# A two-layer megakernel on 2048 tokens: the last chunk of 512 split into two of 256

## What is computed

```
x = ln(x + mamba(x))                    # recurrence of 256 channels x 16 states along each sequence
x = ln(x + fp8_linear(x))
x = ln(x + ssm(x))                      # recurrence of 16 states, one delta per token
x = ln(x + moe(x))                      # 8 experts, top 2, capacity 512 per expert, plus a side net

def mamba(x):
    xi, res = split(x @ in_proj.T)
    xi = silu(causal_conv4(xi))
    dt, B, C = split(xi @ x_proj.T)
    delta = softplus(dt @ dt_proj.T + b)
    h[t] = exp(delta[t] * A) * h[t-1] + delta[t] * B[t] * xi[t]      # per channel and state
    y = sum over states of h[t] * C[t] + xi * D
    return (y * silu(res)) @ out_proj.T

def moe(x):                             # every expert is applied to every token here,
    h = rms(x)                          # and weighted with its routing weight, mostly zero
    out_e = (gelu(h @ Wg[e]) * (h @ Wu[e])) @ Wd[e]
```

## Time and profile before

| | us |
|---|---|
| median of 3 runs | 455.78 |
| lowest and highest run | 454.69, 455.82 |
| the profiled execution, its own time | 457.87 |
| its span, first to last instruction | 456.1 |
| mean granted TensorE clock | 0.945 of full speed |
| busy: TensorE, VectorE | 406.6 (89%), 380.9 (84%) |
| busy: ScalarE, GpSimd | 316.4 (69%), 257.7 (57%) |
| table loads of ScalarE | 66, 84.7 in all |

### The profile page before, as it was taken

The page is one execution under the profiler, slowest core; times in us unless marked ns, Lnnn a source line. Parts: engine busy times, 40 slices in busy tenths (PEclk is TensorE's granted clock), DMA queues, the critical chain, the costliest instruction groups (busy, mean ns, idle before and its releaser), DMA issues.

```text
span 456.1 us, 6082 instructions
## 1 busy us (share of the span) xinstructions
PE 406.6 (89%) x1700; PEld 245.5 (54%) x1700; DVE 380.9 (84%) x849; ACT 316.4 (69%) x524; POOL 257.7 (57%) x230
## 2 busy tenths in 40 slices
PE   9969977688676999999999899999978998999993
PEld 5323422243223568866354477675434865868872
DVE  3599998999998999999999899999897566657654
ACT  2787637267954768887889999899672779566331
POOL 0348899999899744766865199978592000000000
PEclk9988989799789799999999899999988999999997
DMA  8397597786773925655652852757440000000000
GB/s 264 144 384 264 213 324 308 278 290 220 239 251 124 283 91 181 198 171 185 216 176 92 266 207 90 276 185 227 166 138 0 2 1 0 1 2 23 1 0 23
DMA packets 22208, 74.18 MB, mean 163 GB/s; under 512 B 2336, under 2 KB 4512, under 8 KB 21792
## 3 DMA queue, kind: packets, MB, share of 16 engines
q1 hardware_dynamic: 22176, 73.82, 47.8%
HBM read 72.50 MB, written 1.31 MB: 162 GB/s over the span
## 4 chain that ended last, share of the span: by engine, by line
PE 61%; DVE 15%; ACT 14%; issue 9%; POOL 1%; DVEq 0%; ACTq 0%; POOLq 0%
PE ps_y L659 14%; PE ps_net L753 14%; PE ps_acc L799 9%; DVE ps_state L1263 4%; DVE product L1280 3%; PE ps_net L619 3%; ACT ps_state L945 3%; PE ps_state L753 3%; ACT L817 2%; PE ps_y L799 2%; PE ps_net L624 1%; PE ps_y L652 1%; DVE acc L1445 1%; ACT sp_abs L821 1%; DVE drive L1263 1%
## 5 line engine op out<-in xcount | busy, mean ns | idle before, releaser
L1109 POOL TENSOR_TENSOR drive<-du,b_row 128x512 f32<-128x512 f32 x128 | 164.5, 1308 | 28.3 <-DVE ps_state L1263 15.6
L659 PE MATMUL ps_y<-product,par 128*128 128x512 f32 x256 | 136.3, 655 | 16.8 <-DVE product L1280 11.5
L945 ACT ACTIVATE ps_state<-delta,decay_rate 128x512 f32<-128x512 f32 x128 | 84.0, 681 | 39.6 <-DVE product L1280 34.4
L659 PEld LDWEIGHTS ps_y<-product,par 128*128 128x128 f32 x256 | 49.8, 208 | 78.1 <-issue 37.4
L817 ACT ACT_TABLE_LOAD x66 | 84.7, 1283 | 1.9 <-PEq L1519 0.7
L1138 POOL TENSOR_TENSOR product<-drive,c_row 128x512 f32<-128x512 f32 x42 | 53.4, 1272 | 26.0 <-DVE drive L1263 25.9
L799 PEld LDWEIGHTS ps_acc<-wd,hidden 128*128 128x128 f32 x448 | 53.8, 192 | 7.4 <-issue 4.7
L1280 DVE TENSOR_TENSOR product<-ps_state,c_row 128x512 f32<-128x512 f32 x86 | 57.1, 676 | 0.1
L1263 DVE TENSOR_TENSOR_SCAN ps_state<-ps_state,drive 128x512 f32<-128x512 f32 x46 | 54.5, 1212 | 2.2 <-ACT ps_state L945 1.1
L799 PE MATMUL ps_acc<-wd,hidden 128*128 128x128 f32 x448 | 54.9, 276 | 0.2 <-DVE acc L1445 0.2
L753 PE MATMUL ps_net<-hn_part,wg 128*128 128x512 f32 x165 | 51.6, 435 | 3.0 <-DVE picked L1396 1.8
(11 more groups left out here) (199 smaller groups left out, 499.5 us busy)
## 6 DMA issues: line engine op xcount, KB each, us to landing
b_row<-bc_dram SPq DMA_DIRECT2D x64, 512.0 KB, 5.1
c_row<-bc_dram SPq DMA_DIRECT2D x64, 512.0 KB, 4.2
x_in<-x_t SPq DMA_DIRECT2D x4, 256.0 KB, 9.2
gelu<-w_gate SPq DMA_DIRECT2D x1, 1024.0 KB, 8.9
hidden<-w_up SPq DMA_DIRECT2D x1, 1024.0 KB, 11.0
wd<-w_down SPq DMA_DIRECT2D x1, 1024.0 KB, 11.2
out<-acc SPq DMA_DIRECT2D x4, 256.0 KB, 2.3
par<-params SPq DMA_DIRECT2D x1, 598.0 KB, 7.0
```

The source lines that it names most:

```text
L659: mm(ps_y[:, :], ident, product[:, g % PRODUCTS, :], start=False, stop=(n == STATE - 1)).then_inc(y_pe, 1)
L945: nc.scalar.activation(ps_state[g % RING][:, :], delta[:, c % 2, h, :], ACT.Exp, scale=decay_rate[:, h, n:n + 1]).then_inc(decay_act, 1)
L1109: nc.gpsimd.tensor_tensor(drive[:, g % DRIVES, :], du[:, h, :], b_row[:, m % ROWS, n % 2, :], ALU.mult).then_inc(drive_pool, 1)
```

## The change

The chunks get a table of sizes, 512, 512, 512, 256, 256, and starts. Every stage takes its width `w` and its number of 128-token blocks `nb` from it, in place of `CHUNK` and `BLOCKS`. The second sequence now has three chunks (2, 3 and 4), so chunks 2 and 3 keep their last states (`KEEPS`), where before chunk 2 did. `LAST` is now chunk 4. Buffers keep their sizes. `PLACES` is new as a whole, with numbers for chunk 4; of it one line stands here. The other edits repeat the pattern shown.

```diff
-CHUNKS = TOKENS // CHUNK
-PER_BATCH = LENGTH // CHUNK
+SIZES = (512, 512, 512, 256, 256)
+CHUNKS = len(SIZES)
+STARTS = tuple(sum(SIZES[:c]) for c in range(CHUNKS))
+FIRST = tuple(t % LENGTH == 0 for t in STARTS)
+KEEPS = tuple((t + w) % LENGTH != 0 for t, w in zip(STARTS, SIZES))
...
-PAIRED = (NONE, NONE, NONE, NONE)
+PAIRED = (NONE,) * CHUNKS
 QUARTER = frozenset(range(3, UNITS, 4))
-MULTIPLIED = (QUARTER, QUARTER, THIRD, ODD)
+MULTIPLIED = (QUARTER, QUARTER, THIRD, ODD, ODD)
...
-        "split": (0.2025, 0.4051, 1.0127, 1.2152, 2.6338999999999997, 2.6344, 2.6348999999999996, 2.6353999999999997, 2.6358999999999995, 2.6363999999999996, 2.6369, 2.6373999999999995,),
+        "split": (0.1612, 0.3224, 0.4836, 0.6448, 0.9673, 1.1285, 1.2897, 1.4509, 1.6121, 1.7733, 1.9345, 2.0957),
...
-                mm(ps_y[:, :], ident, product[:, g % PRODUCTS, :], start=False, stop=(n == STATE - 1)).then_inc(y_pe, 1)
+                mm(ps_y[:, 0:w], ident, product[:, g % PRODUCTS, 0:w], start=False, stop=(n == STATE - 1)).then_inc(y_pe, 1)
...
-                nc.scalar.activation(ps_state[g % RING][:, :], delta[:, c % 2, h, :], ACT.Exp,
+                nc.scalar.activation(ps_state[g % RING][:, 0:w], delta[:, c % 2, h, 0:w], ACT.Exp,
...
-                    for j in range(BLOCKS):
+                    for j in range(nb):
...
-                    load_x(2)
-                    load_x(3)
+                    for i in range(2, CHUNKS):
+                        load_x(i)
```

More of the change, by code:

```diff
@@ L499, in carried @@
             eng.wait_ge(carry_pool if multiplied(g) else carry_dve,
-                        sum(which(i) for i in range(g + 1) if i // UNITS % PER_BATCH == 0))
+                        sum(which(i) for i in range(g + 1) if KEEPS[i // UNITS]))
         def blocks_of(ap):
-            return ap.rearrange("p (j d) -> p j d", j=BLOCKS)
+            return ap.rearrange("p (j d) -> p j d", d=P)
         def run(engine, **parts):
@@ L638, in pre @@
                     low_made(pe, c)
-                    last = mm(bank_[:, :], dt_proj[0:RANK, h * P:(h + 1) * P], low[0:RANK, :], start=True, stop=True)
+                    last = mm(bank_[:, 0:w], dt_proj[0:RANK, h * P:(h + 1) * P], low[0:RANK, 0:w], start=True, stop=True)
                 last.then_inc(pre_pe.sem, 1)
             def finish(c, k):
+                w, nb = SIZES[c], SIZES[c] // P
                 g = c * UNITS + k
@@ L679, in tail @@
                     after(pe, tail_act, c, "x1")
-                    for j in range(BLOCKS):
-                        last = turn(block_of(ps_tail[:, :], j), x1[:, j, :], ident)
+                    for j in range(nb):
+                        last = turn(block_of(ps_tail[:, 0:w], j), x1[:, j, :], ident)
                     last.then_inc(tail_pe.sem, 1)
@@ L684, in tail @@
                     after(pe, tail_act, c, "x1q")
-                    for j in range(BLOCKS):
-                        last = mm(block_of(ps_tail[:, :], j), x1_q[:, j * P:(j + 1) * P], ffn_q[:, :], start=True, stop=True)
+                    for j in range(nb):
+                        last = mm(block_of(ps_tail[:, 0:w], j), x1_q[:, j * P:(j + 1) * P], ffn_q[:, :], start=True, stop=True)
                     last.then_inc(tail_pe.sem, 1)
@@ L689, in tail @@
                     after(pe, tail_act, c, "x2")
-                    for j in range(BLOCKS):
-                        last = turn(block_of(ps_tail[:, :], j), x2[:, j, :], ident)
+                    for j in range(nb):
+                        last = turn(block_of(ps_tail[:, 0:w], j), x2[:, j, :], ident)
                     last.then_inc(tail_pe.sem, 1)
@@ L715, in tail @@
                     after(pe, tail_act, c, "hn")
-                    for j in range(BLOCKS):
-                        last = turn(block_of(ps_tail[:, :], j), hn[:, j, :], ident)
+                    for j in range(nb):
+                        last = turn(block_of(ps_tail[:, 0:w], j), hn[:, j, :], ident)
                     last.then_inc(tail_pe.sem, 1)
```

325 lines of the change are left out of this document (180 added, 145 removed), and 248 rows, old and new, of the table PLACES.

## The result

The changed kernel takes 473.7 us (median of 4 runs, 472.0 to 474.4), the kernel before in the same job 455.8 (454.7 to 457.7): ratio 1.038, 95% interval 1.034 to 1.043. The forecast was 473.0. The profiled execution of after took 473.18 us, its span 471.3.

A forecast was written before the change was run, and what follows sets the result against it. It took VectorE to bound the recurrence before and ScalarE after the change. Recurrence end at 408 plus 65 behind it gave 473.5 against span 456.1, hence a 473 us median; range 456 to 490.

The forecast's parts named there:

- (a): Behind the recurrence, tail 4, net 4 and the last norm together take 65 us in place of 103.8, a gain of 38.8.
- (b): From chunk 2's start to the recurrence's end, VectorE's work grows by 42.6 us, from 162.0 to 204.6.
- (c): Over the same recurrence stretch, ScalarE's work grows from 144.9 to 217 us, with 28 more table loads, and passes VectorE.
- The forecast's own test: Inside the recurrence, VectorE's idle time before scans released by an exponential, a few us before, must grow clearly.
- (d): From chunk 2's start to the recurrence's end: busiest engine keeps its 93% share, so 217 / 0.93 = 233 us, ending at 408.
- (e): Other engines and chunks 0 and 1: pair loads stay hidden, GpSimd is not the bound, TensorE's work stays the same in sum.
- The start of the stretch: Chunk 2's recurrence starts 3 us earlier, at 175 instead of 177.9, as four joins and four accumulations move from chunk 1.
- R1: In the recurrence, table loads fall where ScalarE waited anyway and VectorE stays the bound: stretch 220, total 459.5 us; chance 0.20.
- R2: Waits inside the recurrence vanish and the shorter end outweighs everything: stretch 211, total 448 us; chance 0.10.
- R3: In chunks 3 and 4, three half-width states ahead are too few: up to 1.4 us lost per excursion, total 488; chance 0.15.

## Why the prediction was right, and where it was not

- **(a) Behind the recurrence: right.** Tail 4 took 33.9 us (36 forecast, bounds 30 and 42). Net 4 took 24.0 (441.3 to 465.3, 22.5 forecast) and the last norm 6.0 (6.5 forecast). 63.9 in sum against 65. Three 256-column matmuls take 0.35 to 0.36 us in the chain of waits, half of three at 512, as assumed.
- **(b) VectorE in the stretch: right within some 2%.** 208.9 us measured, 204.6 forecast. A half-width scan starts 0.65 us after the one before (0.625 forecast, bounds 0.59 and 0.71).
- **(c) ScalarE in the stretch: right as a sum, wrong as a cause.** 215.6 us measured, 217 forecast, with the 94 loads forecast. It did pass VectorE. But 79 us of it taken away moved the end of the recurrence by 1.3 us. The forecast's own test, that VectorE's idle time behind exponentials must grow clearly or (d) is wrong, came out against it: 1.8 us.
- **(d) The length of the stretch: right number, wrong engine.** The step says: "In before the engine with most work is busy 162.0 of 95.5 + 78.9 = 174.4 us, 93%." That is VectorE. The row it comes from the earlier trace rows has TensorE at 91.94 + 74.67 = 166.6 us, 95.5%. I had sorted the engines by who waits for whom in the recurrence and passed over the larger number. The rule itself (the busiest engine keeps its share) held in all kernels of the table within some 4 points.
- **(e) The rest: here the work was lost.** "TensorE's work is the same in sum" was nearly true of the kernel (411.6 against 406.6) and false of the stretch, where it rose by 57.0 to 223.6 us. By step (d)'s own rule with TensorE, 223.6 / 0.955 = 234 us. ScalarE's 217 / 0.93 = 233 gave the same end by luck, since both engines' work had grown to nearly the same sum. Had the gelus needed no table loads, the forecast would have been some 220 us for the stretch, by VectorE, and 14 us too short.
- **The start of the stretch: a smaller miss.** 172.4 instead of 175, and more of net 0 moved out of chunk 1 than the four joins and four accumulations counted: TensorE's work there fell by 10.3 us. That the one made the other is likely and not shown.
- **The rivals.** R1 (the tables hidden, VectorE the bound, stretch 220) was right that the loads are hidden, but TensorE's 223.6 us alone are more than its 220. (The share of ScalarE that it names, 0.85, is 144.9 / 174.4 = 0.83.) R2 needed waits inside the recurrence to vanish. R3 (the ring too short, up to 1.4 us lost per excursion) has 1.8 us in all to show for itself; the starts of chunks 3 and 4, which it named as well, may be part of the some 10 us of new TensorE idle time, which I can't divide further.

The Trainium skill ("Perfetto Trace Analysis", Identifying the Most-Contended Engine) ranks engines by their busy share, but judges TensorE by the share of the peak rate that it reaches and by its weight loads' busy time, and not by its matmuls'. By the weight loads (57.44 + 45.87 = 103.3 of 174.4 us, 59%) TensorE would have come behind VectorE, as in the forecast; by the matmuls' it comes first. The runs with the loads or VectorE's accumulations away bear out the latter; the run with cheaper product sums, where 24.4 us less of TensorE's work gained 1.0, shows that this share isn't the whole answer either.

## What to carry to other kernels

When work moves from one stage to another, write down every engine's work in both stages before and after the move, TensorE's too, even if its total doesn't change: here a stage lasted its busiest engine's work and 5 to 9% more, and one whose busiest engine was at 95% had no room to hide anything. A narrower last chunk does shorten the end (by about 23 us here), but it costs the narrow operations (6 to 8 us for the halved chunk) and brought the neighbour's work into a full stage. Whether the split pays with an order that leaves net 2 where it was, no run shows. And where the right time comes out, take the supposed cause away once before believing in it.

## What the runs showed of the hardware

- With float32r product sums TensorE was granted 0.56 of its clock where it had 0.88 (64 to 95 us), and 0.74 where it had 0.90 over the first 178 to 180 us. By my estimate the edit should have saved 79 us of busy time; it saved 47 (359.5 us busy against 406.6). So part of what cheaper matmuls save can go back to a lower clock on an engine that already waits.
- A change of table on ScalarE costs 1.28 us of the engine, and taking 79 us of such loads out of the stretch of after shortened it by 0.5 us. That the exponentials run up to three states ahead may be why; it wasn't tested.
- A scan over 128x256 takes 0.735 to 0.742 us against 1.272 for 128x512, and 0.65 against 1.18 from start to start; exponentials 0.466 us against 0.681. Half the columns cost 55 to 68% of the time.
